# Pair counts of a graph kernel: one wait per four items for a free bank, and ten registers loaded per eight items in place of sixteen

## The reference

```python
x = layernorm(x + L0(x))   # two ARMA convolutions: 3 stacks, 2 steps each, sums over edges weighted by degree
x = layernorm(x + L1(x))   # GCN: out[d] = sum over edges s->d of (x@W)[s] * dinv[s] * dinv[d]
x = layernorm(x + L2(x))   # relational GCN, 9 edge types, both directions, 2 layers
x = layernorm(x + L3(x))   # out[d] = (sum over edges s->d of x[s]) @ Wn.T + x[d] @ Ws.T + biases
```

## Time and profile before

| what | value |
|---|---|
| median of three executions | 5177.45 us |
| the profiled execution: its time | 5171.15 us |
| the profiled execution: its span, first to last instruction | 5169.9 us |
| the stage of the pair counts in it, first register load to last matmul's block taken | 677.0 to 952.0 us |
| granted TensorE clock, mean over the span | 0.782 |

### The profile page before, as it was taken

How to read it: one execution, slowest core, us unless ns; L and a number is a source line. 1 busy time by engine, 2 the same in 40 slices (tenths; PEclk the granted TensorE clock), 3 DMA queues, 4 the chain that set the end, 5 groups by cost and what they waited for, 6 DMA issues and landing times. The chain is left out here.

```text
span 5169.9 us, 61002 instructions
## 1 busy us (share of the span) xinstructions
PE 3797.4 (73%) x17060; PEld 2393.7 (46%) x17062; DVE 2488.8 (48%) x3871; ACT 969.2 (19%) x2696; POOL 1922.2 (37%) x2046
## 2 busy tenths in 40 slices
PE   5978765699999959999987866676667544444459
PEld 2534422256555524544444555565555433333344
DVE  7989977405888851111233744344345522222221
ACT  2937646323000031111121000000001000000011
POOL 0000000003677600000000467777772777777730
PEclk7979989899999979999988865555558755555569
DMA  0000023516888725255423612222224422222214
GB/s 17 0 0 0 0 102 152 195 64 219 291 295 293 244 68 172 90 172 167 139 95 119 227 46 53 52 53 53 53 53 178 136 52 53 52 53 53 53 60 133
DMA packets 152021, 556.42 MB, mean 108 GB/s; under 512 B 40992, under 2 KB 49537, under 8 KB 151628
## 3 DMA queue, kind: packets, MB, share of 16 engines
q0 software_dynamic: 87216, 288.32, 18.4%
q1 hardware_dynamic: 64278, 265.76, 14.4%
q10 hardware_dynamic: 390, 0.60, 0.0%
HBM read 442.68 MB, written 111.85 MB: 107 GB/s over the span
## 5 line engine op out<-in xcount | busy, mean ns | idle before, releaser
L2109 PE MATMUL ps_sum_rgcn<-gathered_rgcn,select_sum_rgcn 128*128 x3328 | 996.0, 447 | 686.5 <-DMA gathered_rgcn<-by_dst,row 369.6
L2109 PEld LDWEIGHTS ps_sum_rgcn<-gathered_rgcn,select_sum_rgcn 128*128 128x128 f32 x3328 | 776.3, 313 | 762.3 <-issue 757.9
L2024 POOL DMA_INDIRECT gathered_rgcn<-by_dst,row x782 | 740.8, 947 | 238.3 <-issue 233.2
L2024 POOL DMA_INDIRECT gathered_rgcn<-by_src,row x686 | 647.3, 944 | 245.4 <-issue 202.4
L712 PE MATMUL ps_sum_arma<-gathered_sum_arma,select_sum_arma 128*128 128x384 f32 x1664 | 551.9, 491 | 20.9 <-DMA gathered_sum_arma<-arma,other 18.6
L698 POOL DMA_INDIRECT gathered_sum_arma<-arma,other x416 | 393.3, 945 | 430.6 <-POOLq L784 260.8
L1624 PE MATMUL ps_sum_arma<-pair_counts_sum_arma,parts_sum_arma 128*128 128x512 f16 x2625 | 539.6, 361 | 14.0 <-DVE outT_arma_mid L2249 5.8
L2465 POOL DMA_INDIRECT gathered_rgcn<-by_src,row x96 | 92.3, 962 | 1161.3 <-POOLq L784 1132.7
L2178 DVE TENSOR_TENSOR select_sum_rgcn<-one_hot_sum_rgcn,ps_coef_sum_rgcn 128x2048 f32<-128x2048 bf16 x52 | 119.0, 2288 | 680.0 <-PE ps_sum_rgcn L2109 679.9
L712 PEld LDWEIGHTS ps_sum_arma<-gathered_sum_arma,select_sum_arma 128*128 128x128 f32 x1664 | 308.5, 190 | 264.1 <-issue 62.9
L746 DVE TENSOR_TENSOR acc_arma_end<-acc_arma_end,ps_sum_arma 128x768 f32 x416 | 396.9, 954 | 57.4 <-PE ps_sum_arma L712 35.8
(11 more groups left out here) (447 smaller groups left out, 5108.0 us busy)
## 6 DMA issues: line engine op xcount, KB each, us to landing
pair_counts_sum_arma<-pairs SPq DMA_DIRECT2D x125, 800.0 KB, 4.3
by_src<-rows_rgcn_src_table SPq DMA_DIRECT2D x50, 576.0 KB, 2.8
by_dst<-rows_rgcn_dst_table SPq DMA_DIRECT2D x50, 576.0 KB, 3.8
exact<-whole_pairs SPq DMA_DIRECT2D x25, 800.0 KB, 3.4
pairs<-whole_pairs POOLq DMA_DIRECT2D x25, 800.0 KB, 5.1
pair_counts_sum_x<-pairs SPq DMA_DIRECT2D x25, 800.0 KB, 4.4
pair_counts_sum_gcn<-pairs SPq DMA_DIRECT2D x25, 800.0 KB, 4.3
air_counts_sum_neighbour<-pairs SPq DMA_DIRECT2D x25, 800.0 KB, 4.3
```

Of the source, the lines that this page charges most:

```text
L2024: nc.gpsimd.indirect_dma_start(got[:, n % PLACES, :], None, table, bass.IndirectOffsetOnAxis(ap=o.row[:, n % C:n % C + 1], axis=0)).then_i ...
L2109: nc.tensor.matmul(ps[:, bass.ds(slot, P)], select[:, parity, u, :], rows[:, bass.ds(place, D)], start=False, stop=False, skip_group_check ...
```

## The change

The table gets one row of ten integers per eight items: eight columns of banks, and two numbers of banks that must be free, one for each four items. They are those of the fourth and the eighth item; as the block never falls, they cover the other three. PE loads ten registers per eight items, and waits for `freed` once per four items, on the instruction that carries the wait for `made`. The matmuls themselves, and all that DVE, ACT, SP and POOL do in this stage, stay as they were. A row is 40 bytes long.

```diff
+FOUR = 4
+OCTET = 2 * FOUR
+ROW = OCTET + 2
@@ staircase_stage
-            nc.vector.tensor_scalar(items[:, :, 1], b_at[:, :], 1.0, None, ALU.add)
+            nc.vector.tensor_scalar(q.item_at[:, :, OCTET:ROW],
+                                    b_at[:, :].rearrange("p (n h a) -> p n h a", h=2, a=FOUR)[:, :, :, FOUR - 1], 1.0, None, ALU.add)
...
-            nc.vector.tensor_scalar(items[:, :, 0], tile_at[:, :], float(SPAN), None, ALU.mult)
+            nc.vector.tensor_scalar(q.item_at[:, :, 0:OCTET], tile_at[:, :].rearrange("p (n a) -> p n a", a=OCTET),
+                                    float(SPAN), None, ALU.mult)
@@ pair_counts_stage
+        item_at = q.item_at[:, :, :].rearrange("p n a -> p (n a)")
...
                 for u in range(2 * V):
-                    if u % 8 == 0:
-                        table = load(PE, q.item_at, i * (4 * V) + 2 * u, 16, (SPANS - 1) * SPAN)
-                    if u % 4 == 0:
-                        pe.wait_ge(made, i * (2 * V) + u + 4)
-                    pe.wait_ge(freed, table[u % 8 * 2 + 1])
-                    nc.tensor.nop(nofuse=True)
-                    nc.tensor.matmul(ps[:, bass.ds(table[u % 8 * 2], SPAN)], source[:, u // V, u % V // 2, :, u % 2],
+                    if u % OCTET == 0:
+                        table = load(PE, item_at, i * (2 * V // OCTET * ROW) + u // OCTET * ROW, ROW, (SPANS - 1) * SPAN)
+                    if u % FOUR == 0:
+
+                        pe.wait_ge(made, i * (2 * V) + u + FOUR)
+                        pe.wait_ge(freed, table[OCTET + u % OCTET // FOUR])
+                        nc.tensor.nop(nofuse=True)
+                    nc.tensor.matmul(ps[:, bass.ds(table[u % OCTET], SPAN)], source[:, u // V, u % V // 2, :, u % 2],
                                      target[:, u % V, :], start=False, stop=False, skip_group_check=True).then_inc(multiplied, 1)
@@ adjacency
-        q.item_at = c.sb("item_at", [P, 2 * ITEMS], I32)
+        q.item_at = c.sb("item_at", [P, ITEMS // OCTET, ROW], I32)
```

More of the change, by code:

```diff
@@ L1270, in staircase_stage @@
         chunk_at = sb("chunk_at", [P, ITEMS])
-        items = q.item_at[:, :].rearrange("p (n a) -> p n a", a=2)
         ps = c.psum("ps", [P, 8, 512])
@@ L1918 @@
 SLOTS = 2
-OCTET = U // 2
 STEPS = C // U
```

## The result

| | before | changed |
|---|---|---|
| median of eight executions | 5173.77 us (5168.7 to 5179.24) | 5188.68 us (5181.93 to 5198.17) |
| ratio, with its 95% interval | | 1.0032 (1.0021 to 1.0043) |
| the profiled execution's span | 5169.9 us | 5180.6 us |
| PE's sequencer in the stage, first register load to last branch | 677.0 to 951.2 us | 677.5 to 962.2 us |

What follows compares the result with a forecast made beforehand. The prediction took PE's sequencer to bound the stage: waits -43, dearer register loads +36 and more slowing of loads under stores +12 sum to +5 us, so 5177.45 becomes 5182 us, range 5160 to 5215.

Steps and rivals of the forecast that it cites:

- PE's sequencer is the bound and never waits: In the pair-count stage, PE's instruction sequencer sets the 274 us pace; waits put down to ACT or DVE are coincidences.
- The waits, -43 us: In PE's stage loop, 432 waits removed at 0.10 us each save 43 us (bounds -22 and -52).
- Ten registers: dear in every second octet, by the address: PE's table loads: rows starting off 16 bytes load registers singly, 2.19 us; rows on 16 bytes 1.02 us.
- The size of that, +36 us: PE's 72 ten-register loads average 1.605 us in place of 1.107, adding 36 us in quiet (bounds -37 and +78).
- The stretch, +12 us: PE's register loads slowed while a tile's stores run: more accesses caught, 42 us in place of 30.8 (bounds 0, +45).
- The matmuls at 0.22 us, also below: PE's matmuls take 1.73 us per eight items, below the sequencer's need, so they add no time.
- The coarser wait, 0: Waiting for free banks once per four items costs PE nothing (bound +25); as a rival, late banks, 5207, chance 0.05.
- DVE's table write, 0: DVE's smaller table write stands before 9.62 us of idleness: 0, up to 1 us without that cover.
- rows by fours everywhere: Rival on PE's table loads: only the count matters, 1.02 us each, giving 5128 us, or 5106 if proportional; chance 0.16.
- all rows singly: Rival on PE's table loads: every row loads its registers singly, 2.19 us each, giving 5232 us; chance 0.04.
- The stores catch the singles: Rival on PE's loads under stores: long single-register loads nearly always touch a store, giving 5201 to 5215 us; chance 0.15.

Runs made afterwards that it cites:

- e2: Kernel before with only one wait for a free bank per four items, its table and sixteen-register loads kept: -39.1 us, ratio 0.9934 against the kernel before.
- e3: Changed kernel with a wait before each item put back, ten-register loads and 40-byte rows kept: +54.1 us, ratio 1.0096 against the kernel before.
- e6: Changed kernel with 80-byte rows, one load of twenty registers per sixteen items: -79.9 us, ratio 0.9861 against the kernel before.
- e1: Changed kernel with rows padded to 48 bytes, still ten registers per load: -39.4 us, ratio 0.9924 against the kernel before.
- e4: Changed kernel with its table begun 4 bytes later, so every row is off 16 bytes: +60.4 us, ratio 1.0108 against the kernel before.
- e8: Kernel before with its table begun 8 bytes later, still sixteen registers per load: +224.0 us, ratio 1.0402 against the kernel before.
- e9: Changed kernel unedited, measured again beside the kernel before on the first comparison's chip: +22.1 us, ratio 1.0037.
- e7: Changed kernel with most of the exact store (integer copy of the matrix) left out: -11.9 us, ratio 0.9980 against the kernel before.
- e5: Changed kernel with 48-byte rows and twelve registers per load, the two counts written twice: -62.4 us, ratio 0.9900 against the kernel before.

## Why the prediction was right in kind and short in size

The forecast was +5 us (5182), too small to be told from no change; measured are +14.9 (5188.68), inside the range, but slower by more than 0.2%, which had a chance of 0.27. Point by point:

- **PE's sequencer is the bound and never waits**: right (its last branch takes 76 ns and is over at 951.2, not 951.3, which changes nothing). What is taken from it or given to it goes to the stage's time, less or plus what the stretch grows by (e2: -45 in the sequencer, -33 in the stage; e3: +46 and +57), and in e6 the bound moves to DVE, near the 192 us named (197).
- **The waits, -43 us**: right, 45 in the trace (0.105 us each), 33 net of stretch in e2's stage.
- **Ten registers: dear in every second octet, by the address**: right; the two kinds came in turn (1.08 and 2.41 us), and e1, e4 and e8 turn them on and off.
- **The size of that, +36 us: the step that failed.** It measures +46. I took the price of a single register from ACT's loads, 215 ns; on PE it is 234 (e4, e8). An odd octet's ten singles cost 2.41 us in place of 2.19, and the even rows, with two singles, 1.08 in place of 1.02. The forecast gave no range for that price between two engines, though PE's loads were to be had only by fours. No run has the same count of singles on both engines, so that it is the engine which makes the price is the likely reading and not a tested one.
- **The stretch, +12 us**: right in size, +10 in this profile, but by luck in part. I let it grow with the number of accesses, 14 in two octets in place of 8. It grows by as much where that number stays at four a load (e2: 43 us against 31.6, e1: 43), and the dearer loads then add next to nothing to it (41.6 in this profile, 44.7 in e9's). In all the traces the stretch is 0.58 to 0.66 of the time that loads and stores share, by fours or singly, so what counts is how much of the stage is spent in loads. In the sum it happened to fit.
- **The matmuls at 0.22 us, also below**: this holds at the upper clock level alone. At the lower one they take 0.43 us each, 3.4 an octet, more than the sequencer's 3.3 (1.54 and a mean load of 1.75). The forecast had left that out; it costs 1.6 us at the stage's end, as said below.
- **The coarser wait, 0**: right (e2). **DVE's table write, 0**: nothing speaks against it; the stage begins at 677.5 us in place of 677.0, but with the same table code it began at 677.8 in e9 and 678.8 in e7, so such a difference is that of one execution from another.
- **What the sum still lacked**: the matmuls' own end. The sequencer explains +10.5 of the +14.9. It now ends with matmuls still queued behind it, as the weight loads of the last octet show, 0.43 us apart (changed kernel, timeline, and windows from 960 to 965, where the granted clock is 0.54, near the lower level):

```profile
961.81 0.15 PEld L1456 LDWEIGHTS ps_pairs<-target_one_hot_pairs,source_one_hot_pairs 128*128 128x128 f16 x1 [0.28 <-issue]
...
963.09 0.15 PEld L1456 LDWEIGHTS ps_pairs<-target_one_hot_pairs,source_one_hot_pairs 128*128 128x128 f16 x1 [0.28 <-issue]
963.52 0.15 PEld L1456 LDWEIGHTS ps_pairs<-target_one_hot_pairs,source_one_hot_pairs 128*128 128x128 f16 x1 [0.28 <-issue]
```

```profile
960.00:965.00 5.00, 3.59 (x8) 1.11 (x8) 0.00 (x0) 0.33 (x2) 0.00 (x0) 0.54 0.00 0
```

  The last branch is over at 962.2 and the last matmul starts at 963.95, where before they fell at 951.2 and 951.3: +1.6 us, an octet that the sequencer issues in 1.5 us and PE needs 8 x 0.43 for. The other 3 us lie between the medians and a single profile: the executions of the changed kernel spread over 16 us, and the stretch alone differs by 3 us between its two profiles.

The rival "rows by fours everywhere" (0.16) is refuted by the odd loads of the changed kernel and by e4, "all rows singly" by its even loads and by e1. "The stores catch the singles" overstated a cost: it begins above the forecast's 42 us of stretch, and 41.6 was measured.

## What to carry to other kernels

Where a stage is paced by a sequencer, look at its own records: constant steps between them, whatever the other engines do, show that it is the bound, and every instruction taken out counts (0.105 us for a wait here, before the 12 us that the stretch took back in e2). Price a register load by where it begins before counting its registers: pad the rows of a table to a multiple of 16 bytes, and round the count up to a multiple of four rather than down. Then fewer, longer loads are worth most until the next engine's floor is met; here that made 80 us of a change that lost 15.

## What the runs showed of the hardware that I had not expected

- Twelve registers load faster than ten from the same rows (848 against 1084 ns), and sixteen off the 16 bytes take 3.8 us against 1.107 (e5, e1, e8). (The Trainium skill, Runtime: NRT & Kernel Launch, Instruction fetch mechanics, gives about 200 ns per register for a TENSOR_LOAD. The page describes these as loads from HBM, so it does not settle the price of the loads from SBUF here, which the prediction set against it as if it did. Off the 16 bytes the runs come near it, with 238 to 241 ns per register on PE; on them they do not, with 67 to 108.)
- A single cost 215 ns on ACT (loads of five and seven registers) and 234 on PE (ten and sixteen).
- Register loads are slowed by stores of other queues that run at the same time: up to 5.2 us for one that takes 2.4 in quiet, and about half of the stretch goes when half of the bytes go (e7: 22.3 us against 41.6).
